# A recommendation tower on one core: first table loads moved to SP, weight splits behind the gram copies, the last gathered field handled alone, and the last stores dealt out by chunk

## The reference

```
e = stack([tbl_f[ids[:, f]] for f in range(26)], axis=1)         # 2048 x 26 x 128
combined = concatenate([dense[:, None, :], e], axis=1)           # 2048 x 27 x 128
inter = einsum('bfd,bgd->bfg', combined, combined)               # 2048 x 27 x 27
z = concatenate([dense, inter[:, iu, ju]], axis=1)               # pairs above the diagonal
h = concatenate([z, dense], axis=1)
h = maximum(h @ W_top1 + b_top1, 0)                              # 607 -> 512
h = maximum(h @ W_top2 + b_top2, 0)                              # 512 -> 256
y = h @ W_top3                                                   # 256 -> 1
```

## Time and profile before

| what | value |
|---|---|
| median of 3 runs | 361.67 us (361.46 to 362.02) |
| profiled execution, whole | 362.94 us |
| its span, first to last instruction | 361.1 us |
| mean granted TensorE clock | 0.981 |
| PE matmul busy | 326.2 us, 90% |
| DVE busy | 240.6 us, 67% |
| ACT busy | 183.1 us, 51% |
| POOL busy | 251.3 us, 70% |

### The profile page before, as it was taken

How to read it: one execution, slowest core, us unless ns; L and a number is a source line. 1 busy time by engine, 2 the same in 40 slices (tenths; PEclk the granted TensorE clock), 3 DMA queues, 4 the chain that set the end, 5 groups by cost and what they waited for, 6 DMA issues and landing times.

```text
span 361.1 us, 10388 instructions
## 1 busy us (share of the span) xinstructions
PE 326.2 (90%) x4192; PEld 313.6 (87%) x4192; DVE 240.6 (67%) x721; ACT 183.1 (51%) x359; POOL 251.3 (70%) x268
## 2 busy tenths in 40 slices
PE   0486686999999999999999999999999999999676
PEld 0375685999999999999999999999899999999575
DVE  4799956897649962995479763995299555951011
ACT  1346553447645574456633763556544664366414
POOL 5777777777777777777777777777777777772410
PEclk9999997999999999999999999999999999999969
DMA  5999558674245524662446424552466344520220
GB/s 148 258 246 244 134 155 218 142 193 104 77 113 142 147 68 111 118 189 80 98 106 170 124 69 109 128 179 68 100 121 191 80 100 98 131 67 24 42 69 0
DMA packets 47469, 44.80 MB, mean 124 GB/s; under 512 B 26138, under 2 KB 41498, under 8 KB 47422
## 3 DMA queue, kind: packets, MB, share of 16 engines
q1 hardware_dynamic: 38140, 25.86, 29.3%
q0 software_dynamic: 8448, 17.04, 19.2%
q10 hardware_dynamic: 834, 1.24, 1.4%
HBM read 39.33 MB, written 4.78 MB: 122 GB/s over the span
## 4 chain that ended last, share of the span: by engine, by line
PE 82%; DVE 7%; DMA 7%; ACT 2%; SPq 1%; issue 1%; ACTq 0%
PE ps_o L330 39%; PE ps_m L367 16%; PE ps_g L356 14%; PE ps_t L341 7%; DVE onehot L724 4%; DMA oh_ids<-onehot_ids 3%; DVE tbl_lo L709 2%; PE ps_m L397 2%; DMA interaction_scratch<-inter 1%; DMA x<-w_dense 1%; DMA x<-interaction_scratch 1%; SPq L205 1%; PE ps_o L412 1%; PE ps_g L427 1%; PE ps_t L412 1%
## 5 line engine op out<-in xcount | busy, mean ns | idle before, releaser
L309 POOL DMA_INDIRECT rows<-tables,idx x256 | 246.3, 962 | 80.4 <-issue 76.5
L724 DVE TENSOR_SCALAR onehot<-oh_ids,rownum 125x256 fp32r<-125x256 int32 x640 | 199.9, 387 | 51.1 <-PE ps_o L330 46.6
L330 PE MATMUL ps_o<-onehot,tbl_hi 125*128 125x256 f32 x640 | 162.5, 293 | 21.9 <-DVE tbl_lo L709 21.9
L330 PE MATMUL ps_o<-onehot,tbl_lo 125*128 125x256 f32 x640 | 158.1, 286 | 0.0
L330 PEld LDWEIGHTS ps_o<-onehot,tbl_hi 125*128 125x128 f32 x640 | 124.8, 195 | 26.5 <-DVE tbl_lo L709 23.8
L330 PEld LDWEIGHTS ps_o<-onehot,tbl_lo 125*128 125x128 f32 x640 | 125.1, 195 | 0.0
L536 ACT ACTIVATE emb<-ps_o 128x256 f32<-128x256 f32 x80 | 49.3, 738 | 91.2 <-PE ps_o L330 91.2
L356 PE MATMUL ps_g<-emb 128*54 128x54 f32 x2048 | 57.7, 217 | 5.3 <-ACT inter L567 4.1
L356 PEld LDWEIGHTS ps_g<-emb 128*54 128x54 f32 x2048 | 55.0, 132 | 8.5 <-ACT inter L567 4.4
L552 ACT ACTIVATE emb<-ps_t 128x512 f32<-128x512 f32 x64 | 46.3, 726 | 10.9 <-PE ps_t L341 10.6
L567 ACT ACTIVATE inter<-ps_g 128x432 f32<-128x432 f32 x64 | 33.8, 531 | 17.0 <-PE ps_g L356 14.9
(11 more groups left out here) (55 smaller groups left out, 209.1 us busy)
## 6 DMA issues: line engine op xcount, KB each, us to landing
oh_ids<-onehot_ids SPq DMA_DIRECT2D x80, 128.0 KB, 4.0
rows<-tables,idx POOLq DMA_INDIRECT x256
x<-interaction_scratch SPq DMA_DIRECT2D x23, 117.0 KB
inter<-small_tables SPq DMA_DIRECT2D x4, 448.0 KB
interaction_scratch<-inter SPq DMA_DIRECT2D x30, 47.2 KB
interaction_scratch<-inter SPq DMA_DIRECT2D x32, 38.2 KB
interaction_scratch<-inter SPq DMA_DIRECT2D x28, 42.2 KB
dense<-dense_e SPq DMA_DIRECT2D x8, 128.0 KB, 3.6
```

The source lines that it names most:

```text
L309: pool.indirect_dma_start(rows[e][:, k, :], None, tables[k], bass.IndirectOffsetOnAxis(ap=idx[:, NG * hh + k:NG * hh + k + 1], axis=0),).t ...
L330: mm = pe.matmul(o, tbl[p][:, k, c, :], onehot[n % SLOTS_OH][:, c, :], start=(c + p == 0), stop=(c == TCHUNKS - 1 and p == 1))
L724: op = nc.vector.tensor_scalar(onehot[n % SLOTS_OH][:, c, :], oh_ids[0:TPART, n % IDS, :], rownum[:, c:c + 1], None, ALU.is_equal)
```

## The change

Four edits, none of which changes what is computed.

1. The loads of the first two tables, which ACT issued once the first gather ids had landed, are issued by SP, each directly behind the first and second one-hot ids; tables 2 and 3 and the identity follow them.
2. In the first block ACT copies the grams of both halves before it splits the dense weights. DVE builds one-hot 11 and 12 one place earlier, each ahead of a weight split.
3. The very last gather (field 15 of half 15) has a semaphore of its own. PE transposes the three fields before it as one group and the last alone, into another PSUM bank; ACT copies them in two instructions.
4. Of the last block's stores, the wrapped part moves from POOL to ACT, in front of the second-layer ReLUs of block 6; POOL stores only band 2, and waits for band 0 to have landed first. ACT issues the load of chunk 0 ahead of the copy of block 6's result.

```
-        def store_wrapped(eng, i, quads, stored):
+        def store_wrapped(eng, i, quads):
...
-                if i == LAST and b >= 2:
-                    eng.wait_ge(last_stored[b], 16 * QUAD)
+                if (i, b) == (LAST, 2):
+                    eng.wait_ge(last_stored, 16 * QUAD)
...
             load_ids(0)
+            load_stage(sp, 0)
             load_ids(1)
-            load_stage(sp, 2)
+            load_stage(sp, 1)
             load_ids(2)
             sp.dma_start(ident[:, :], identity).then_inc(ident_loaded, 16)
+            load_stage(sp, 2)
             load_stage(sp, 3)
...
-                        ).then_inc(gathered[e][g], 16)
-            store_wrapped(pool, LAST, range(QUAD), last_stored)
+                        ).then_inc(last_gathered if (hh, k) == (HALVES - 1, NG - 1) else gathered[e][g], 16)
+
+            pool.wait_ge(inter_stored[0], 16 * QUAD * BLOCKS)
             store_band(pool, LAST, 2, range(QUAD), last_stored)
...
+            def last_transposes():
+
+                e, g, (s, n) = 1, NGR - 1, GROUPS[-1]
+                q = NGR * HALVES - 1
+                pe.wait_ge(gathered[e][g], 16 * (n * BLOCKS - 1))
+                pe.wait_ge(rows_placed, q - 1)
+                for k in range(n - 1):
+                    mm = pe.transpose(ps_t[q % 2][:, 128 * k:128 * (k + 1)], rows[e][:, s + k, :],
+                                      ident[:, :])
+                mm.then_inc(transposed, 1)
+                pe.wait_ge(h1_ready, 2 * K1 * LAST)
+                pe.wait_ge(last_gathered, 16)
+                pe.transpose(ps_m[1][:, 0:128], rows[e][:, NG - 1, :], ident[:, :]).then_inc(last_transposed, 1)
...
-                transposes(b, 3)
+                last_transposes()
                 grams(b)
...
+            def place_last_rows():
+                s, n = GROUPS[-1]
+                q = NGR * HALVES - 1
+                act.wait_ge(transposed, q + 1)
+                src = ps_t[q % 2][:, 0:128 * (n - 1)].rearrange("d (k r) -> d r k", r=128)
+                nc.scalar.activation(emb_view(1)[:, :, 1 + s:s + n], src, ACT.Copy)
+                act.wait_ge(last_transposed, 1)
+                nc.scalar.activation(emb_view(1)[:, :, NG], ps_m[1][:, 0:128], ACT.Copy).then_inc(rows_placed, 1)
...
             def first_body():
-
-                act.wait_ge(idx_loaded[0], 16)
-                load_stage(act, 0)
-                load_stage(act, 1)
                 for k in range(4):
                     split_hi(k)
...
                 copy_grams(0)
                 split_hi(NO + 1)
+                copy_grams(1)
                 split_hi(DENSE_ITEM)
-                copy_grams(1)
                 split_hi(DENSE_ITEM + 1)
...
-                place_rows(b, 3)
+                place_last_rows()
                 copy_grams(b)
-                store_band(act, LAST, 0, range(2, QUAD), inter_stored)
+                store_band(act, LAST, 0, range(2, QUAD), inter_stored[0])
+                store_wrapped(act, LAST, range(QUAD))
                 relus2(m)
+                load_x(act, LAST, 0)
                 copy_y(m)
-                load_x(act, LAST, 0)
...
             make_onehot(NO)
+            make_onehot(NO + 1)
             split_lo(NO)
-            make_onehot(NO + 1)
+            make_onehot(NO + 2)
             split_lo(NO + 1)
             add_dense_weights()
-            make_onehot(NO + 2)
             split_lo(DENSE_ITEM)
```

More of the change, by code:

```diff
@@ L127, in build_tower @@
         rows_placed = sem("rows_placed")
+        last_gathered = sem("last_gathered")
+        last_transposed = sem("last_transposed")
         gram_done = sem("gram_done")
@@ L130, in build_tower @@
         inter_stored = [sem(f"inter_stored{b}") for b in range(WRAPPED + 1)]
-        last_stored = [sem(f"last_stored{b}") for b in range(WRAPPED + 1)]
+        last_stored = sem("last_stored")
         x_loaded = [sem(f"x_loaded{c}") for c in range(XCHUNKS)]
@@ L188, in store_band @@
                 eng.dma_start(scratch[f0:f1, f0 + 1:g1, q, :],
-                              inter[p + f0:p + f1, col + f0 + 1:col + g1, :]).then_inc(stored[b], 16)
-        def store_wrapped(eng, i, quads, stored):
+                              inter[p + f0:p + f1, col + f0 + 1:col + g1, :]).then_inc(stored, 16)
+        def store_wrapped(eng, i, quads):
             f0 = SHIFTS + 1
@@ L197, in store_wrapped @@
                 eng.dma_start(scratch[f0:FEATURES, FEATURES:WRAP, q, :],
-                              inter[p + f0:p + FEATURES, col:col + SHIFTS, :]).then_inc(stored[WRAPPED], 16)
+                              inter[p + f0:p + FEATURES, col:col + SHIFTS, :]).then_inc(inter_stored[WRAPPED], 16)
         def load_stage(eng, n):
@@ L242, in turn_interactions @@
                 for b in range(len(BANDS)):
-                    store_band(sp, i, b, range(QUAD), inter_stored)
-                store_wrapped(sp, i, range(QUAD), inter_stored)
+                    store_band(sp, i, b, range(QUAD), inter_stored[b])
+                store_wrapped(sp, i, range(QUAD))
                 load_ids(NO * (i + 1) + NO - 1)
@@ L290, in _ @@
             load_x_dense(LAST)
-            store_band(sp, LAST, 0, range(0, 2), inter_stored)
-            store_band(sp, LAST, 1, range(QUAD), inter_stored)
+            store_band(sp, LAST, 0, range(0, 2), inter_stored[0])
+            store_band(sp, LAST, 1, range(QUAD), inter_stored[1])
             for c in range(1, PAIR_CHUNKS):
```

## The result

The changed kernel takes 359.73 us (median of 20 runs, 358.67 to 362.03) and the kernel before, run beside it, 361.45 (20 runs): a ratio of 0.9947, 95% interval 0.9926 to 0.9968. The changed kernel is faster, by 0.3 to 0.7%, but by some 1.7 us and not by the forecast 4.8. 359.73 lies outside the range of 355.4 to 359.1. The profiled execution took 359.83, with a span of 358.0 and a mean granted clock of 0.986.

What follows compares the result with a forecast made beforehand. PE bounds the kernel, with POOL's gathers a second chain about as long. Span 361.1 - 5.5 (last grams earlier) + 0.7 (stores) = 356.3; with 1.84 around it 358.1, less 1.27 to the median: 356.9 us, range 355.4 to 359.1.

Steps and rivals of the forecast that it cites:

- the head: Start of the kernel through block 1: edits 1 and 2 together gain 6.4 us (5.1 to 8.2).
- the prediction's own signs of being wrong: PE never waits for a gather; POOL's last gather over 1 us from 326.2; last gram copy to end changes over 2.
- the third rival: Late ids or late DVE in block 1: head gives 3.4, edit 3 nothing, last grams at 331.5; 359.0 us, chance 0.09.
- Edit 2: forecast 5.4: First block: PE's stop of 3.58 us and the slow clock after it go; PE gains 5.4.
- Edit 1: forecast +1.0: DVE's early waits for table 0 and ids: gain between 0 and 2.5 us, taken as 1.0; a loss unlikely.
- The upper end of 2.5: Edit 1's largest gain, if DVE's waits of 2.11 for table 0 and 0.34 for ids both go.
- The meeting with the gathers: Last field: PE ready at 327.1, last gather lands at 328.6, so PE waits 1.5 us; last grams at 329.4.
- a few tenths: How far the first 60 us can move POOL, whose last gather starts at 326.19.
- Edit 3: forecast 0.5: Last group of fields: splitting off the last field cuts landing to last grams from 1.35 to 0.8, worth 0.5.
- Edit 4: forecast a loss of 0.7: Last stores: wrapped stores hold ACT and delay chunk 0's load; between gain 0.5 and loss 2.0, taken as loss 0.7.
- The step from the trace to the median: The profiled execution stands 1.27 us above the median of the runs; this is taken off the forecast of 358.1.
- the prediction's 1.46 and 0.93: Clock loss after PE's first-block stop: 1.46 us on 64 gram matmuls, 0.93 on block 1's first 32 lookups.

Runs made afterwards that it cites:

- run 1: The changed kernel without edit 1 (ACT loads tables 0 and 1 again): 359.65 us, ratio 0.9938 to the kernel before.
- run 2: The kernel before with edit 2 alone (gram copies ahead of the dense weights' split, one-hots one place earlier): 359.43 us, ratio 0.9924.
- run 7: The kernel before with edit 1 alone (first tables loaded by SP behind the first ids): 363.26 us against 361.92, ratio 1.0038.
- run 3: The changed kernel with the fourth one-hot's ids ahead of tables 2 and 3 in SP's queue: 359.11 us, ratio 0.9908.
- run 8: The kernel before with edit 2 and the second layer's low part split later on DVE, without edits 1, 3 and 4: 359.86 us, ratio 0.9928.
- runs 5 and 6: The changed kernel without edit 1 and with the second layer's low part behind block 0's x splits, 359.51 us; the same also without edit 3, 359.74.

## Why the prediction was wrong

The direction was right, but the forecast failed at the head, which gave 3.11 and not 6.4, so that PE never met the last gather. Two of the prediction's own signs of being wrong came true: in the changed kernel's trace PE waits for no gather, and POOL's last gather starts 1.10 from where it was. What came true was the third rival, "the head falls short", with last grams at 331.5 (331.69 measured), its 359.0 (0.7 too low), its cause ("the third and fourth ids come later", "block 1 finds DVE late") and its consequence that edit 3 gives nothing. I gave it 0.09. The steps of the forecast in turn:

- **Edit 2: forecast 5.4, measured 4.42** (runs 1 and 2). Its own place came as worked out: no stop, full clock, one-hot 13 at 59.22. The step that I left out is the next instruction in DVE's row. The low part of the second layer's weights had found its high part ready (ACT split it at 63.22 in the trace before); with one-hot 13 at 59.22, 5.64 earlier, it waits 1.15. 5.64 - 1.15 leaves 4.49, and 4.42 was measured. This is the question "what is late next", which I put to DVE only as far as one-hot 13.
- **Edit 1: forecast +1.0, "a loss is unlikely"; measured -1.31 in head** (81.66 against 80.35), and no gain alone (run 7). This is the step that failed in its sign. The bytes were the same, but their order was not: the ids that DVE needs next were issued behind both tables, at 7.45 instead of 6.13, and landed 1.1 later, while table 0, which came sooner, was not what paced DVE; with these ids ahead of tables 2 and 3 the loss is gone (run 3). The size is that of this pair of traces: in run 7's the ids came early and nothing shows as lost. The Trainium skill ("DMA: Bandwidth & Descriptors", section "Issuing engines are not separate DMA queues") would have had about nothing from it; the runs show somewhat less than nothing. The upper end of 2.5 also left out a third wait of DVE, 0.32 us ahead of its third one-hot at 14.42.
- **The head: 6.4 forecast, 4.42 - 1.31 = 3.11 measured.**
- **The meeting with the gathers: found, but too late and at the wrong place.** I had PE meet the last gather at 328.6 and wait 1.5 there. Run 8 had the head of the forecast, and its last fields came at 330.75, 2.1 later than that. Two things were mis-sized. The last gather's start, 326.19 in the earlier trace rows, was one execution's value, which I allowed "a few tenths"; ten other traces with all gathers and POOL's start as it is or 0.3 earlier have 325.64 to 328.18. And PE meets POOL in the last group of fields of an earlier block (3 to 6), where the landing took 3.2 (in block 6 of run 2) and not 2.4. What is lost there can't be taken back at the last field: from one such group to the next PE works 39.6 us anyway (290.28 to 329.88 in run 2). What I overlooked is that POOL is the slower of the two in every block: the last gathers of halves 13 and 15 of run 2 start 40.24 apart (287.07 and 327.31), while PE goes from one block's first layer to the next in 39.42 (81.66 to 121.08 in the changed kernel). PE draws nearer to the gathers by some 0.8 us a block, and the longer landing of block 6 makes its distance there as small as in the last block (none and some 0.2 us in run 2, with the 2.4 of the changed kernel's trace for the last landing).
- **Edit 3: forecast 0.5, measured nothing** (runs 5 and 6). Its premise, a wait at the last field, didn't come about even with the fast head. The landing itself, 2.4 after the start, was estimated rightly.
- **Edit 4: forecast a loss of 0.7; 0.09 between the two traces, 0.6 between means of traces.** The mechanism is in the trace: ACT held for 3.94, the ReLUs late, chunk 2 copied 13.31 after the start of the last gram copy where it was 11.92. Chunk 0, which the term went by, was copied only 0.2 later (8.75 against 8.55). What the late chunk 2 costs is nearly covered by PE's clock: before, it was low from the wait for chunk 0 until PE was through most of chunk 1, so that PE reached chunk 2 late; after the change it is full again before chunk 0's matmuls (stages of before and after, which are 6.6 to 10.6 and 9.8 to 13.8 us behind the last gram copy; columns as in the earlier trace rows):

```profile
345.00:349.00 4.00, 1.96 (x9) 1.67 (x9) 0.43 (x1) 0.42 (x1) 0.00 (x0) 0.50 0.31 79
```

```profile
345.00:349.00 4.00, 3.36 (x29) 3.15 (x28) 0.47 (x2) 0.83 (x2) 0.00 (x0) 1.00 0.18 50
```

- **The step from the trace to the median: 1.27 taken off, 0.10 measured.** I treated the distance of the profiled execution from the median as a constant. But it was in part what the change itself affects: that execution, at clock 0.981, had paid the clock loss behind PE's stop, which run 7's trace doesn't pay, and which edit 2 removes. That this makes up the distance is likely, not shown.

The miss of 2.8 is made up of 1.7 of span (358.0 against 356.3: last grams 2.3 later than forecast, end 0.6 sooner behind them) and 1.2 from that subtraction.

What stays open: how much edit 4 costs, and why POOL's gathers run some 2 us faster or slower in all from one execution to the next. The traces place this in the gathers themselves: their busy time adds up to 245.7 us in run 1 and 248.2 in run 8, while the idle time before them is the same (80.5 in both). What makes single gathers longer, up to 1.96 where 0.945 is usual, isn't shown.

## What to carry to other kernels

Where two engines run side by side through the whole program, find their smallest distance over all blocks and over several executions, not at the last block of one, and compare what each of them takes per block: a gain at the start stops being one at the first place where it is used up. When a stall is removed, follow the row of every engine in that stretch to the next wait. And before a load is moved ahead on a queue, ask which of the loads now behind it is the one that paces the consumer.

## What the runs showed of the hardware

The time of the kernel before goes with the mean granted clock of each execution. Of 35 runs in one group, eight at a mean clock of 0.981 have a median of 364.47 us, ten at 0.986 have 362.04, and nine at 0.990 have 360.43. Of the changed kernel's 20 runs, three at 0.981 have 359.98, six at 0.986 have 359.38, seven at 0.990 have 359.11 and four at 0.995 have 359.95: no such slope. In the two traces that have PE's stop in the first block, it cost nothing beyond its own length (3.64 us, run 7) and some 2.4 us (3.58 us, the prediction's 1.46 and 0.93). That the changed kernel is steadier fits its having no such stop; the gathers may hold it too, which isn't shown.

The four wrapped stores, 42 KB each in runs of 256 bytes, held ACT for 3.94 us; issued by POOL (run 8) the same four took 2.51. ACT's two stores of band 0 just ahead of them took 0.92 together; what then holds it isn't shown.
